# Keys and values of the fourth attention formed inside the third expert stage, kept in DRAM and split by batch

## The reference

```
for l in 0..3:
    x = x + tanh(g_xattn[l]) * attention_l(layernorm(x), ctx)
    x = x + tanh(g_ffn[l])   * experts_l(layernorm(x))
```

```
xn = layernorm(x, ln_gamma, ln_beta)          # x is normalized already: a second norm
q = xn @ w_q                                  # 256 x 256 by 256 x 1024, per batch
k, v = split(context @ w_kv)                  # the context doesn't change from layer to layer
attn = softmax(q k^T / 8)                     # per head
out = (attn @ v) @ w_out + b_out, times tanh(gate)
```

## Time and profile before

| what | value |
|---|---|
| time, median of 3 runs | 3298.18 us (3293.73 to 3299.65) |
| span of the profiled execution | 3289.2 us; the page gives no other time for it |
| busy, share of the span | TensorE 79%, VectorE 48%, ScalarE 39%, GpSimd 37% |
| third expert stage | about 1717 to 2261 us of the span |
| fourth attention, its batches | 2325 to 2801 us |

### The profile page before, as it was taken

The page is one execution under the profiler, slowest core; times in us unless marked ns, Lnnn a source line. Parts: engine busy times, 40 slices in busy tenths (PEclk is TensorE's granted clock), DMA queues, the critical chain, the costliest instruction groups (busy, mean ns, idle before and its releaser), DMA issues. The chain is left out here.

```text
span 3289.2 us, 56555 instructions
## 1 busy us (share of the span) xinstructions
PE 2598.4 (79%) x18079; PEld 2371.2 (72%) x18080; DVE 1586.2 (48%) x3706; ACT 1270.1 (39%) x3125; POOL 1213.7 (37%) x1139
## 2 busy tenths in 40 slices
PE   5674388399979999579982799990899999799993
PEld 4564387289968888479972678880788988688882
DVE  3665455566534444446541233434567766343232
ACT  3231144044533333135532334430566766333331
POOL 0012562654124833310005456605243443256313
PEclk9786699599969999769985899995899999799996
DMA  3031263200002532210002233402000000033212
GB/s 111 0 128 46 91 183 117 79 21 15 8 30 78 154 94 81 61 33 21 15 11 67 89 111 115 119 24 64 7 13 7 6 13 1 26 110 113 87 64 87
DMA packets 127505, 205.86 MB, mean 63 GB/s; under 512 B 16400, under 2 KB 88364, under 8 KB 127136
## 3 DMA queue, kind: packets, MB, share of 16 engines
q1 hardware_dynamic: 63232, 117.84, 11.9%
q10 hardware_dynamic: 50208, 47.31, 4.6%
q0 software_dynamic: 13824, 37.53, 3.6%
HBM read 145.58 MB, written 57.02 MB: 62 GB/s over the span
## 5 line engine op out<-in xcount | busy, mean ns | idle before, releaser
L490 ACT ACTIVATE moe_act<-moe_gu 128x256 f32<-128x256 f32 (+1 forms) x431 | 189.6, 440 | 613.6 <-PE moe_gu L95 613.6
L93 PE MATMUL moe_gu<-moe_whi,moe_xThi 128*128 (+2 forms) x1018 | 410.2, 403 | 9.8 <-POOL moe_wlo L289 9.8
L93 PE MATMUL moe_yp<-moe_whi,moe_hThi 128*128 (+1 forms) x1238 | 391.5, 316 | 8.2 <-DVE moe_hTlo L772 7.9
L95 PE MATMUL moe_gu<-moe_whi,moe_xTlo 128*128 (+2 forms) x1018 | 389.7, 383 | 0.0
L94 PE MATMUL moe_gu<-moe_wlo,moe_xThi 128*128 (+2 forms) x1018 | 388.9, 382 | 0.0
L289 POOL TENSOR_TENSOR moe_wlo<-moe_raw,moe_whi 128x768 fp32r<-128x768 f32 (+1 forms) x170 | 341.1, 2007 | 37.0 <-issue 13.4
L94 PE MATMUL moe_yp<-moe_wlo,moe_hThi 128*128 (+1 forms) x1238 | 348.9, 282 | 0.0
L95 PE MATMUL moe_yp<-moe_whi,moe_hTlo 128*128 (+1 forms) x1238 | 348.0, 281 | 0.0
L772 DVE TENSOR_TENSOR moe_hTlo<-moe_tp,moe_hThi 128x256 fp32r<-128x256 f32 (+1 forms) x431 | 210.4, 488 | 232.6 <-ACT moe_hThi L496 231.5
L756 DVE TENSOR_TENSOR moe_h<-moe_act,moe_gu 128x256 f32<-128x256 f32 x321 | 135.0, 421 | 378.4 <-ACT moe_act L490 358.6
L314 POOL DMA_INDIRECT moe_whi<-rows_y,moe_slot_r x144 | 138.7, 963 | 380.4 <-DMA rows_y<-moe_y 337.8
(11 more groups left out here) (457 smaller groups left out, 6875.6 us busy)
## 6 DMA issues: line engine op xcount, KB each, us to landing
moe_raw<-in_moe_w SPq DMA_DIRECT2D x118, 384.0 KB, 3.2
moe_raw<-in_moe_w SPq DMA_DIRECT2D x52, 512.0 KB, 4.3
moe_xr<-rows_x ACTq DMA_DIRECT2D x69, 256.0 KB, 2.8
rows_y<-moe_y ACTq DMA_DIRECT2D x69, 256.0 KB, 2.2
rows_x<-att_zeros SPq DMA_DIRECT2D x16, 512.0 KB, 6.7
att_cT_hi<-ctxT_hi SPq DMA_DIRECT2D x24, 256.0 KB, 2.7
att_cT_lo<-ctxT_lo SPq DMA_DIRECT2D x24, 256.0 KB, 3.0
moe_xr<-rows_x ACTq DMA_DIRECT2D x41, 128.0 KB, 2.1
```

The source lines that it names most:

```text
L93: pe.matmul(out, lhs[0], rhs[0], start=first, stop=False, **kw)
L95: return pe.matmul(out, lhs[1], rhs[0], start=False, stop=last, **kw)
L490: act.activation(act_sb[i % 2][:, :], gu[i % 2][:, 0:HC], func).then_inc(act_done, 1)
```

## The change

The fourth attention's K and V don't depend on `x`. The change forms them in the third expert stage: 64 products, 8 a batch, four of K and four of V, of 128 x 512 each. Four stand behind the logits, 36 behind the ranks, 24 after the last expert's results. ScalarE copies each from PSUM and issues a store of 256 KB to `kd` or `vd` in DRAM (fp32). Their weights (8 pieces) are split ahead of expert 0's. The context tiles share SBUF with the turned rows, and the copies with the second slot of the expert weights, so expert 1's weights, the first `turn_x` and the load of the first rows come behind the first 40. In `heads_phase` the K and V rounds are gone; SyncE loads 1 MB of K and 1 MB of V a batch; GpSimd casts the high half of a 128 x 512 part, VectorE forms the low half. The batch loop is written out for all eight batches. In `place`, a register operation by block is added in all expert stages.

```diff
@@ heads_phase, tables
-        ROUNDS = [(4, "nT", 0), (5, "nT", 1), (6, "qT", 0), (7, "kT", 0), (8, "qT", 1), (9, "kT", 1), (10, "V0", 0), (10, "qT", 2),
-                  (11, "kT", 2), (12, "V0", 1), (13, "qT", 3), (14, "kT", 3)]
-        OWN = [(2, "V1", 0), (3, "V1", 1)]
+    BODY = [(4, "nT", 0), (5, "nT", 1), (6, "qT", 0), (8, "qT", 1), (10, "qT", 2), (13, "qT", 3)]
+    K_AT = {7: 0, 9: 1, 11: 2, 14: 3}
+    V_AT = {2: (0, 2), 3: (0, 3), 10: (1, 0), 12: (1, 1)}
+        k_raw = w["k"][0][:, :, :].rearrange("p k (c s) -> p (k c) s", s=S)
+        def halves_at(h, last):
+            found = []
+            if h in K_AT and not last:
+                found.append(("k", 1, K_AT[h]))
+            if h in V_AT and not (last and V_AT[h][0]):
+                found.append(("v", *V_AT[h]))
+            return found
@@ heads_phase, sync
+                def load_k(i, lo, turn):
+                    wait(sp, kl_done, i, lo, 4, 4 * turn)
+                    sp.dma_start(k_raw.bitcast(F32), row_of(G["kd"], i + turn)...).then_inc(k_in, 16)
+                load_k(0, 0, 0)
+                load_v(0, 0, 0)
+                load_k(0, 0, 1)
+                def body(i, lo, hi):
+                    if hi < B - 1:
+                        load_v(i, lo, 1)
+                    if hi < B - 2:
+                        load_k(i, lo, 2)
@@ heads_phase, vector
+                def k_lo(i, lo, turn, part):
+                    wait(v, kh_done, i, lo, 4, 4 * turn + part + 1)
+                    c = slice(2 * part, 2 * part + 2)
+                    v.tensor_tensor(KT[1][:, c, :], k_raw[:, c, :].bitcast(F32), KT[0][:, c, :].bitcast(F32), ALU.subtract).then_inc(kl_done, 1)
+                for part in range(4):
+                    k_lo(0, 0, 0, part)
                 for pos, (_, kind, part) in enumerate(BODY):
                     round_(0, 0, 0, pos, kind, part)
+                for part in range(2):
+                    v_lo(0, 0, 0, part)
...
                         if not (last and h + 2 >= H):
                             inverse(i, lo, h + 2)
                         for pos, kind, part in rounds_at(h, last):
                             round_(i, lo, PRO, pos, kind, part)
+                        for kind, turn, part in halves_at(h, last):
+                            (k_lo if kind == "k" else v_lo)(i, lo, turn, part)
                         if h == 3 and lo > 0:
                             residual(i, lo, -1)
-                run_loop(v, B, CUTS, body)
+                for b in range(B):
+                    body(b, b, b)
@@ heads_phase, gpsimd
+                def k_hi(i, lo, turn, part):
+                    wait(pool, k_in, i, lo, 16, 16 * (turn + 1))
+                    wait(pool, s_ready, i, lo, H, H * turn - H + 4 * part + 4)
+                    c = slice(2 * part, 2 * part + 2)
+                    pool.tensor_copy(KT[0][:, c, :], k_raw[:, c, :].bitcast(F32)).then_inc(kh_done, 1)
...
                             normalize(i, lo, h + 2)
-                        if h == 0 and hi < B - 1:
+                        if h == 0 and not last:
                             norm(i, lo, 1)
+                        for kind, turn, part in halves_at(h, last):
+                            (k_hi if kind == "k" else v_hi)(i, lo, turn, part)
@@ moe_phase
+    AT_LOGITS, AT_ROUTE = (4, 36) if ahead else (0, 0)
+    HEAD, ALL = AT_LOGITS + AT_ROUTE, 8 * B if ahead else 0
+                def context_product(u):
+                    b, j = divmod(u, 8)
+                    bank = kv_ps[u % 4]
+                    if j == 0:
+                        pe.wait_ge(ctx_in[b % 2], 32 * (b // 2 + 1))
+                    if u >= 4:
+                        pe.wait_ge(kv_out, u - 3)
...
+                for u in range(AT_LOGITS):
+                    context_product(u)
                 if not PER:
                     ranks()
+                for u in range(AT_LOGITS, HEAD):
+                    context_product(u)
+                if ahead:
+                    pe.wait_ge(kv_out, HEAD)
...
+                        pe.reg_alu(expert[j], regs[0][j], 0, ALU.max)
...
+                if ahead:
+                    wait_y(pe, NJ - 1)
+                for u in range(HEAD, ALL):
+                    context_product(u)
+                def take_product(u):
+                    act.wait_ge(kv_ready, u + 1)
+                    if u >= 4:
+                        act.wait_ge(kv_stored[u % 4], 16 * (u // 4))
+                    act.activation(kv_sb[u % 4], kv_ps[u % 4][:, :], ACT.Copy).then_inc(kv_out, 1)
...
+                if ahead:
+                    pool.wait_ge(kv_ready, HEAD)
+                    for q in range(4):
+                        pool.wait_ge(kv_stored[q], 16 * (HEAD // 4))
                 for u in range(U0, len(pieces)):
                     split_piece(u)
```

More of the change, by code:

```diff
@@ L227, in moe_phase @@
         store_at = {min(b + PB - 1, NJ - 1): (b, q) for b, q in loads}
-        pieces = []
+        NF = len(first)
+        pieces = list(first)
         for u in range(NE * UE):
@@ L279, in _ @@
                     load_piece(u)
+                if ahead:
+                    sp.wait_ge(dn_done, NI + 1)
+                    for b in range(HEAD // 8, B):
+                        load_ctx(b)
             @block.gpsimd
@@ L392, in _ @@
                 regs = [[pe.alloc_register(f"{name}_{n}{q}") for q in range(NQ)] for n in ("blk", "slot")]
+                expert = [pe.alloc_register(f"{name}_expert{q}") for q in range(NQ)]
                 where = {b: (0, 0) for b in range(SJ)}
@@ L546, in _ @@
                         store_y(*store_at[(i - 3) // NG])
+                take_products(HEAD, ALL)
+                if ahead:
+                    for q in range(4):
+                        act.wait_ge(kv_stored[q], 16 * (ALL // 4))
                 if biases:
@@ L1405, in round_ @@
+                        for t in range(TB):
+                            mm = pe.transpose(bank[:, t * P:(t + 1) * P], n_sb[:, t, part * P:(part + 1) * P], ident[:, :])
+                    else:
+                        if part == 0:
+                            wait(pe, rd_done, i, lo, NRD, a + pos)
                         for c in range(2):
@@ L1480, in round_ @@
-                    wait(act, rd_ready, i, lo, NRD, a + pos + 1)
-                    if small and kind == "v":
-                        wait(act, vh_done, i, lo, 2, 2 * batch)
-                        act.activation(vf[:, :, :], both(bank), ACT.Copy).then_inc(rd_hi, 1)
-                    elif kind == "nT":
-                        if small:
-                            act.activation(nT[0][:, :, :], both(bank), ACT.Copy).then_inc(rd_hi, 1)
-                        else:
-                            act.activation(nT[0][:, part, :], bank[:, 0:S], ACT.Copy).then_inc(rd_hi, 1)
-                    elif small:
+                    batch = (a - PRO) // NRD + 1
@@ L1491, in round_ @@
+                    wait(act, rd_ready, i, lo, NRD, a + pos + 1)
+                    if kind == "nT":
+                        act.activation(nT[0][:, part, :], bank[:, 0:S], ACT.Copy).then_inc(rd_hi, 1)
+                    else:
                         wait(act, s_ready, i, lo, H, H * batch - H + 4 * part + 4)
-                        dst = QT if kind == "qT" else KT
-                        act.activation(dst[:, 2 * part, :], bank[:, 0:S], ACT.Copy).then_inc(rd_hi, 1)
-                    elif kind == "qT":
-                        wait(act, s_ready, i, lo, H, H * batch - H + 4 * part + 4)
+                        both = bank[:, :].rearrange("p (c s) -> p c s", c=2)
@@ L1508, in v_hi @@
-                def v_hi(i, lo, turn, half):
-                    wait(act, v_ready, i, lo, 1, turn + 1)
-                    wait(act, pv_done, i, lo, H, H * turn - H + 8 * half + 8)
-                    for kc in range(KC):
-                        ins = act.activation(v_cols(kc, half, 0), vf_cols(kc, half), ACT.Copy)
-                    ins.then_inc(v_half, 1)
-                for pos, (_, kind, part) in enumerate(ROUNDS):
+                for pos, (_, kind, part) in enumerate(BODY):
                     round_(0, 0, 0, pos, kind, part)
-                if small:
-                    v_hi(0, 0, 0, 0)
@@ L1624, in _, with v_lo @@
+                def v_lo(i, lo, turn, part):
+                    wait(v, vh_done, i, lo, 4, 4 * turn + part + 1)
+                    t, c = v_part(part)
+                    v.tensor_tensor(V[1][:, t, c], v_raw[:, t, c].bitcast(F32), V[0][:, t, c].bitcast(F32), ALU.subtract).then_inc(vl_done, 1)
+                for part in range(4):
+                    k_lo(0, 0, 0, part)
+                for pos, (_, kind, part) in enumerate(BODY):
                     round_(0, 0, 0, pos, kind, part)
-                    if small and kind in ("q", "k"):
-                        laid_lo(0, 0, 0, pos, kind)
```

505 lines of the change are left out of this document (168 added, 337 removed).

## The result

The changed kernel takes 3364.75 us in the median (3355.87 to 3370.6, 4 runs) against 3298.91 us of the kernel before (4 runs; the table above has three of them); the ratio of the runs is 1.018, with an interval of 1.0144 to 1.0216, which is 47 to 71 us. It is slower, as forecast, but by 66 us of the medians and not 22, and all four runs lie above the range of 3285 to 3352.

The account below looks back on a forecast made before the run. TensorE bounds the loop before, a VectorE-GpSimd loop after. Loop and batch 0 +19.6, third expert stage +1.5, register operation +1 make +22 on the median of 3298.2: 3320 us, with 8 in 10 for 3285 to 3352.

Parts of the forecast that it names:

- The waits of VectorE: Fourth attention's loop: VectorE waits for GpSimd's casts, 1.73 us at six slots, 0.3 at slot 10, 7.2 at slot 2.
- What stays of waits: Fourth attention's loop: VectorE's older waits at slots 1, 5 and 6 remain, 3.0 us of its 62.1 a batch.
- The clock: Fourth attention's loop: TensorE's gaps cost about half a clock dip a batch, +0.7 us, for a period of 62.8.
- Rival D: Fourth attention's loop: each gap drops TensorE's clock for several us, 67.6 us a batch, kernel 3349 us; chance 0.09.
- Rival C: Fourth attention's loop: norm's wait costs 3 not 7, two others hide; 55.3 us a batch, kernel 3275; chance 0.09.
- The loop's term: Six batches of the fourth attention go from 58.7 to 62.8 us each, +24.6 us.
- Batch 0: First batch of the fourth attention: six rounds go from the prologue, less new casts, halves and waits: -5.0 us.
- I take +1.5 for both: Third expert stage, head and tail: the 64 products nearly hide in TensorE's idle time; +1.5 us, bounds -1 and +35.
- My own sign of being wrong: Third expert stage: the forecast is wrong if the first expert matmul moves by over 5 us.
- its bound of 7 us and the +1: All four expert stages: the added register operation in place() costs +1 us, 7 if none of it hides.

Follow-up runs that it names:

- The two experiments on the casts: The changed kernel with K and V high halves on ScalarE in place of GpSimd, 3281.11 us; with GpSimd's casts ahead of its normalize, 3293.55 us.
- the doubled scores: The changed kernel with every head's scores in the fourth attention formed twice into the same bank, 12 matmuls in place of 6: 3375.63 us.
- the stage alone: The changed expert stage with the fourth attention of the kernel before, the products' results unused: 3319.88 us, ratio 1.0055 to the kernel before.
- the split alone: The kernel before with the eight K and V weight pieces split ahead of expert 0's and the register operation, no products or stores: 3311.83 us.

## Why the prediction was right in its sign and wrong in its size

**The waits of VectorE: right.** I forecast 1.73 us ahead of each half behind a normalize, 0.3 at slot 10 and 7.2 at slot 2; they are 1.71, 0.42 and 6.05 to 6.89. The two experiments on the casts show that these waits are the cause: without any of them six batches take 323.6 us, and with the one of slot 2 alone 338.6, in place of 395.8. The bound did go from TensorE to the loop of VectorE and GpSimd.

**What stays of waits: the step that failed in the loop.** "What stays: ... Together 3.0" is 1.52 + 0.72 + 1.19 + 1.79 + 0.52 + 0.20 = 5.9 in the batch of 66.4 us. The waits ahead of Q_lo (1.79, forecast 1.74) and at slot 1 (0.52 and 0.20, forecast 0.60) are near what I took; the term that failed is the "about 0.8" behind slot 2, up to the rounds of slot 5, which no row shows: it measured 1.52 + 0.72 + 1.19 = 3.43. I took these waits from batches at full clock. In the changed kernel TensorE comes out of the slot 2 gap at the lower clock, and VectorE waits for scores, p and outputs. At clock 1.00, with the doubled scores, the three are 1.72, so the clock makes about 1.7 of the 2.6 that was missed; the other 0.9 is there at full clock too. With VectorE's work 0.8 longer and 0.9 of gaps too short to be listed, this makes 66.4 - 62.1 = 4.3: 2.9 more in "what stays", 0.3 less in the new waits, 0.8 and 0.9.

**The clock: too small.** I took 0.7 us a batch, half a dip. The granted clock is 0.89 over the whole loop, with two or three falls in every batch. Its price can't be cut out exactly; the run at clock 1.00 bounds it from below, 0.9 us a batch with 11 us of work added, and its three waits behind slot 2 are 1.7 us shorter. That is the same 1.7 as above, counted once. Rival D had the falls right, and its full price of 5.5 is not borne out: everything above 62.1 is 4.3 us. (Rival C's 55.3 a batch, given as with no dip, is 62.8 - 4 - 3.5 and so has the 0.7 of the clock in it; without it the sum is 54.6.) The loop's term, 6 x 4.1 = 24.6, measured 43.5.

**Batch 0: too large a gain.** Of the 7.2 us ahead of the first Q round 4.1 are the stage's tail, as with the stage alone (110.9 - 106.8), and the other 3.1 are put down to the four casts and K_lo ahead of nT_lo; with the casts on ScalarE the 114.0 are about 112. With -4.9 behind, batch 0 gained 1.8 and not 5.0. K_lo's four took 4.11 us where 2.76 was reckoned, beside GpSimd's casts.

**The third expert stage: the edit costed at nothing.** "I take +1.5 for both" measured 8.8 + 2.1 + 4.1 = 15. My sum had no term for the eight pieces' split, and looked for the price at the products and the transfers. At the head those are in fact hidden (first scatter to first turned rows 47.6 us, 46.7 before). What is not is GpSimd's subtract beside VectorE's masks, 8.8 us, which the split alone brings back. My own sign of being wrong, a first expert matmul over 5 us later, has come: against the last logits it is 9.7 us later. In the tail the 24 products, with their loads and stores, are not hidden: the run with the split alone has 106.8 us there, as before, and the one with the whole stage 110.9. GpSimd's gather began 24.5 us after the last turned rows, in place of 23.1, and its 32 issues took 0.5 us longer; the other 2 us lie between the end of the gather and the first Q round, and what makes them was not traced.

**The fourth expert stage: +14.9 against +1, cause open.** The register operation is not it; no row stood behind its bound of 7 us and the +1, and eight more of it showed no cost. In the trace the 14.9 are two halves. TensorE waits 7.7 us longer for loads of rows (18.2 against 10.5 us, the same five places): these took 7.2 to 9.6 us from issue to landing, and 5.7 to 7.7 before. And its own work of the same instructions is 6.8 us longer (369.4 against 362.6 us busy), at a granted clock of 0.96 against 0.98. The five places are the same in all kernels, and the waits longer in those with the new attention written out (16.2 to 18.4 us in six of seven kernels; 13.6 in the one with nine register operations) than in the others (10.5 to 13.5). Writing out the attention of before changed nothing; making the new one a loop took 12 us off. Single profiles stand behind each number. Why the loads take longer, no run shows.

Sum: 15 + 3.1 - 4.9 + 43.5 - 1.4 + 14.9 + 0.4 = 70.6; less the 5.7 of spread ahead of the stage this is the 64.9 of the two profiled executions. My 22 had the mechanism that decides the sign, and a third of the size. The misses are 21 us in the loop and batch 0, 13.5 in the third expert stage and 14 in the fourth.

## What to carry to other kernels

Where a step moves to another engine, ask first behind which instruction of that engine it will stand, and whether that one waits for the engine that will wait for the step: eight casts of 0.6 us a batch cost 57 us over six batches here by their place in one engine's order. Then ask what the longer queue of that engine will run beside, and whether one of the two slows the other, as GpSimd's subtracts did with VectorE's masks. When a loop gets gaps on TensorE, take the waits that remain from rows at the lower clock, not from those at full clock.

## What the runs showed of the hardware

- VectorE's operations on two SBUF tensors of 128x128 took up to 1.87 us in place of 0.29 while a GpSimd subtract of 1.8 us ran, up to 0.96 beside its cast of 0.82, and ended 0.15 us behind it; reductions kept their 0.28. A low half of K took 1.75 in place of 0.69 us in one of its places, beside GpSimd's add_bias; the change made both of its inputs SBUF tiles, where one had been a PSUM bank.
- More work on TensorE, 96 matmuls a batch, made six batches 5.6 us shorter (one profile of each), at a granted clock of 1.00 in place of 0.89.
- Eight more register operations for each block on TensorE's queue cost nothing that could be measured (ratio 1.0192 against 1.018).
- The fourth expert stage, whose own code differs between the kernels by the register operation alone, took 381 to 397 us in twelve profiles, in step with the program around it in some pairs and not in others. In the longest ones its loads of rows landed later and TensorE's granted clock was 0.95 or 0.96, against 0.98 in the shortest.
